# An expert stage of 72 tiles behind an attention stage: 24 of the tiles taken into the last attention steps

## The reference

```
h = [pos_table[pos], nest_table[nesting], seg_table[segments]] @ W        # embedding
h = h + attention(layernorm(h))       # chunks of 128 tokens, 8 heads of 64, feature map exp(q P - max)
h = h + moe(layernorm(h)):
    gates = softmax(x @ Wg + bg);  vals, idx = top_k(gates, 2);  vals /= sum(vals) + 0.01
    y_e = relu(x @ W1[e] + b1[e]) @ W2[e] + b2[e]                         # 8 experts, 128 -> 512 -> 128
    out = sum over the two chosen experts of vals * y_e
```

## Time and profile before

| | us |
|---|---|
| median of the three runs | 421.6 |
| profiled execution, span from first to last instruction | 438.2 |
| TensorE busy | 363.8 (83%) |
| VectorE busy | 313.1 (71%) |
| ScalarE busy | 253.5 (58%) |
| GpSimd busy | 244.2 (56%) |
| mean granted TensorE clock | 0.932 |

### The profile page before, as it was taken

How to read it: one execution, slowest core, us unless ns; L and a number is a source line. 1 busy time by engine, 2 the same in 40 slices (tenths; PEclk the granted TensorE clock), 3 DMA queues, 4 the chain that set the end, 5 groups by cost and what they waited for, 6 DMA issues and landing times.

```text
span 438.2 us, 12358 instructions
## 1 busy us (share of the span) xinstructions
PE 363.8 (83%) x3127; PEld 321.2 (73%) x3127; DVE 313.1 (71%) x1170; ACT 253.5 (58%) x705; POOL 244.2 (56%) x566
## 2 busy tenths in 40 slices
PE   1679999999999999999996435999999999999300
PEld 1457888787787877878885313999999999999300
DVE  7666878788777887777974561777777777678154
ACT  1246677776667676676754101777777777677200
POOL 6111117776667767677677660466666665766500
PEclk9989999999999999999999556999999999999855
DMA  5355500001000000000000031222222222221198
GB/s 136 92 158 159 155 1 21 21 15 31 27 27 13 13 27 27 27 20 13 20 28 28 28 101 48 61 74 73 77 71 76 70 75 70 70 76 58 54 308 243
DMA packets 39227, 29.54 MB, mean 67 GB/s; under 512 B 4679, under 2 KB 35778, under 8 KB 39202
## 3 DMA queue, kind: packets, MB, share of 16 engines
q1 hardware_dynamic: 27858, 16.30, 13.6%
q0 software_dynamic: 4352, 9.45, 6.0%
q10 hardware_dynamic: 6992, 3.50, 2.8%
HBM read 16.50 MB, written 12.73 MB: 67 GB/s over the span
## 4 chain that ended last, share of the span: by engine, by line
PE 63%; DVE 14%; DMA 8%; issue 6%; SPq 5%; DVEq 1%; POOL 1%; ACT 1%; another core or an unknown queue 0%; POOLq 0%; ACTq 0%
PE ps_out L1320 7%; PE ps_oy L1332 7%; PE ps_vc L1332 7%; PE ps_q L1320 6%; PE ps_k L1175 5%; PE ps_out L1213 4%; DMA row_of<-ids_dram 4%; PE ps_oy L1228 4%; PE ps_vc L1175 3%; SPq L480 3%; PE ps_oy L1221 3%; PE ps_q L1175 3%; PE ps_vc L1203 3%; PE ps_ln L1312 2%; PE ps_k L1320 2%
## 5 line engine op out<-in xcount | busy, mean ns | idle before, releaser
L607 POOL DMA_INDIRECT y_dram<-heads_out,place x72 | 73.8, 1025 | 29.9 <-issue 25.9
L578 POOL DMA_INDIRECT slots_dram<-rows,row_id x64 | 63.3, 988 | 19.5 <-issue 19.5
L734 ACT ACTIVATE k_prime<-ps_q,b_T 128x128 f32<-128x128 f32 x108 | 31.8, 365 | 19.8 <-PE ps_q L1320 19.8
L734 ACT ACTIVATE k_prime<-ps_out,b_T 128x128 f32<-128x128 f32 x108 | 31.8, 366 | 19.0 <-PE ps_out L1320 18.9
L544 POOL TENSOR_TENSOR rstd<-moments,ln_eps 128x2 f32<-128x2 f32 x32 | 6.2, 195 | 62.3 <-DVE moments L821 62.1
L1332 PE MATMUL ps_oy<-w_tile,k_prime 128*128 128x128 f32 x288 | 38.1, 275 | 0.4 <-issue 0.4
L1332 PE MATMUL ps_vc<-w_tile,k_prime 128*128 128x128 f32 x288 | 38.1, 275 | 0.1
L1320 PE MATMUL ps_out<-sT,w_tile 128*128 128x128 f32 x288 | 38.1, 275 | 0.0
L539 POOL TENSOR_TENSOR spare<-minus_half,ln_eps 128x2 f32<-128x2 f32 x89 | 18.1, 204 | 35.1 <-ACT heads_out L743 22.1
L1213 PE MATMUL ps_out<-context,qT 128*128 128x130 f32 x256 | 36.1, 283 | 1.5 <-issue 0.8
L1091 DVE COPY w_tile<-w_all 128x640 f32 x72 | 36.0, 499 | 1.5
(11 more groups left out here) (232 smaller groups left out, 1028.2 us busy)
## 6 DMA issues: line engine op xcount, KB each, us to landing
qkv_rows<-slots_dram SPq DMA_DIRECT2D x72, 72.0 KB
w_all<-in_L_ffn_W SPq DMA_DIRECT2D x1, 2048.0 KB, 13.5
w_all<-in_L_ffn_W SPq DMA_DIRECT2D x8, 256.0 KB, 4.6
y_first<-y_dram SPq DMA_DIRECT2D x8, 256.0 KB, 5.6
y_second<-y_dram SPq DMA_DIRECT2D x8, 256.0 KB, 6.0
out<-y_first ACTq DMA_DIRECT2D x8, 256.0 KB, 5.5
y_dram<-heads_out,place POOLq DMA_INDIRECT x72
slots_dram<-rows,row_id POOLq DMA_INDIRECT x64
```

Source lines behind the costliest of these rows:

```text
L578: nc.gpsimd.indirect_dma_start(slots_dram[:, :], bass.IndirectOffsetOnAxis(row_id[:, place_of(p, a), j, k:k + 1], 0), rows[:, place_of(p, ...
L607: nc.gpsimd.indirect_dma_start(y_dram[:, :], bass.IndirectOffsetOnAxis(place[:, a, :], 0), y[:, a, :], None).then_inc(s_placed[a], 16)
L734: last = nc.scalar.activation(hT[:, a % 2, c, :], ps_up[a % 2][0][:, c * P:c * P + P], ACT.Relu, bias=b1_T[:, bass.ds(experts[0] * FC + c, ...
```

## The change

The first 24 tiles of the expert stage (`EARLY = 4 * RING`) are placed from the counts after sequence 11 alone. Full tiles are a region's whole multiples of 128 rows; after 12 sequences there are 6144 choices, 48 tiles' worth, of which at least 41 tiles are full, whatever the routing. A first table (`early_counts`, `early_tiles`, `early_words`) is computed by DVE in steps 14 and 15; a second (`taken_tiles`, `later_counts`, `later_tiles`, `later_words`) places the other 48 tiles, from where the first left off in each region. `sequences` ends at `p = 15`. What steps 16 to 18 did is written out, on each engine, between the first steps of `slot_tile`, by `EarlyTiles`, which runs a given number of them at a time, unrolled. `pad` issues all eight padding DMAs on SP, between the load of tile 11 and that of tile 12; ACT issues none. SP waits for the scatters of sequences 12 to 15 and for the padding only ahead of tile 24. The transposed tile lands in `ps_qT` instead of `ps_ln`, the transposed b1 in `ps_q`. All warm-up matmuls of the expert stage are gone.

```diff
+    EARLY_SEQS = L1 - 2
+    EARLY = 4 * RING
+    LATER = FTILES - EARLY
...
-        for p in range(L1, SEQS + 3):
+        for p in range(L1, SEQS):
...
+    class EarlyTiles:
+        def __init__(self, eng, body, groups=None, known=None):
+            self.eng, self.body, self.groups, self.known = eng, body, groups, known
+            self.next, self.experts = -2, None
+        def run(self, count):
+            for n in range(self.next, self.next + count):
+                if n == EARLY - 2 and self.known is not None:
+                    self.eng.wait_ge(self.known, 2)
+                if n == -2 or n == EARLY - 2 or (n > 0 and n % RING == 0):
+                    self.experts = load_experts(self.eng, self.groups, max(n, 0) // RING)
+                self.body(n, n % RING, n // RING, self.experts(n - max(n, 0) // RING * RING))
+            self.next += count
+        def rest(self):
+            self.run(EARLY - self.next)
...
-        ps_slot, ps_y = ps_ln, (ps_oy, ps_vc)
+        ps_slot, ps_y = ps_qT, (ps_oy, ps_vc)
...
-            pad(sp, 0)
             sp.wait_ge(s_tiles, 1)
             firsts = [sp.value_load(tile_row[0:1, n:n + 1], min_val=0, max_val=SLOTS - P) for n in range(RING)]
-            sp.wait_ge(s_pad, 16 * E)
-            sp.wait_ge(s_empty, 16)
             for a in range(2):
-                sp.wait_ge(s_slots[a], 16 * 2 * TOP * SEQS // 2)
+                sp.wait_ge(s_slots[a], 16 * 2 * TOP * EARLY_SEQS // 2)
...
+            early = EarlyTiles(sp, load_ahead)
+            early.run(2 + RING)
+            pad(sp)
+            early.run(EARLY - 2 * RING)
+
+            sp.wait_ge(s_tiles, 2)
+            sp.wait_ge(s_pad, 16 * E)
+            sp.wait_ge(s_empty, 16)
+            for a in range(2):
+                sp.wait_ge(s_late[a], 16 * 2 * TOP * (SEQS - EARLY_SEQS) // 2)
+            early.rest()
             slot_tiles(sp, load_ahead)
...
+            early = EarlyTiles(pool, place_y)
+            q = SEQS - 3
+            weigh(q, q % 2)
+            pool.wait_ge(s_weighed, q + 1)
+            scatter(q, q % 2, last=1)
+            scale_and_shift(SEQS - 1, 1, moments2, rstd2, shift2, s_mom2, s_rstd2)
+            scatter(q, q % 2, first=1)
+            early.run(3)
+            pool.wait_ge(s_last_weighed, 1)
+            scatter(SEQS - 2, 0)
+            early.run(2)
+            pool.wait_ge(s_last_weighed, 2)
+            scatter(SEQS - 1, 1)
+            early.rest()
...
-            pad(act, 1)
...
+            act.wait_ge(s_groups, 1)
+            early = EarlyTiles(act, slot_tile, group_experts, s_groups)
+            early.run(2)
+            oT_copy(TILES - 1, 1)
+            act.wait_ge(s_late[0], 16 * 2 * TOP)
+            normalize_second(SEQS - 2, 0)
+            early.run(1)
+            x2T_copy(SEQS - 2, 0)
+            early.run(1)
+            normalize_second(SEQS - 1, 1)
+            early.run(1)
+            exps_of(SEQS - 2)
+            x2T_copy(SEQS - 1, 1)
+            early.run(2)
+            exps_of(SEQS - 1)
+            early.rest()
...
+            early = EarlyTiles(dve, slot_tile, group_experts, s_groups)
+            early.run(2)
+            ranks(SEQS - 3, 1)
+            early.run(1)
+            residual(TILES - 1)
+            dve.wait_ge(s_h2, TILES)
+            stats_of(SEQS - 1, stats2)
+            step.wait()
+            moments_of(1, stats2, moments2, s_mom2)
+            early.run(1)
+            gates(SEQS - 2)
+            early.run(1)
+            ranks(SEQS - 2, 0)
+            weigh_last(SEQS - 2, 0)
+            early.run(1)
+            gates(SEQS - 1)
+            early.run(1)
+            ranks(SEQS - 1, 1)
+            weigh_last(SEQS - 1, 1)
+            taken_tiles()
+            early.run(1)
+            later_counts()
+            early.run(1)
+            later_tiles()
+            early.run(1)
+            later_words()
+            early.rest()
...
-            warm_up(12, ps_qT[:, :])
-
...
-                if isinstance(n, int) and -1 <= n < 1:
-                    warm_up(2, ps_qT[:, :])
...
+            pe.wait_ge(s_b1_w, 16)
+            nc.tensor.transpose(ps_b1, b1_rows[:, :], ident[0:E * FC, 0:E * FC]).then_inc(s_b1, 1)
+            early = EarlyTiles(pe, slot_tile)
+            early.run(2)
+            pe.wait_ge(s_b1r, 1)
+            rank_product(SEQS - 3)
+            o_transpose(TILES - 1, 1)
+            early.run(1)
+            y_product(TILES - 1, 1)
+            x2_transpose(SEQS - 2, 0)
+            pe.wait_ge(s_h2, TILES)
+            early.run(1)
+            gate_product(SEQS - 2, 0)
+            early.run(1)
+            rank_product(SEQS - 2)
+            x2_transpose(SEQS - 1, 1)
+            early.run(1)
+            gate_product(SEQS - 1, 1)
+            early.run(1)
+            rank_product(SEQS - 1)
+            early.rest()
             slot_tiles(pe, slot_tile)
```

More of the change, by code:

```diff
@@ L106, in sequences, with load_experts, taken_out, experts @@
             step.base, step.count = start + per * ((L1 - L0) // 2), 0
-        for p in range(L1, SEQS + 3):
+        for p in range(L1, SEQS):
             body(p, p % 2, p // 2)
+    def load_experts(eng, groups, group):
+        if groups is None:
+            return lambda at: None
+        word = eng.value_load(groups[0:1, span(group, 1)], min_val=0, max_val=E ** DIGITS - 1)
+        taken = {}
+        def taken_out(at):
+            if at not in taken:
+                taken[at] = eng.snap((word >> (E_BITS * at)) & (E - 1))
+            return taken[at]
+        def experts(at):
+            return [taken_out(k) if 0 <= k < DIGITS else None for k in range(at, at + 3)]
+        return experts
@@ L130, in load @@
[L130 to L134, removed]
+            return load_experts(eng, groups, group)
         start = step.base + step.count if step else 0
-        with eng.Fori(1, FTILES // RING - 1) as i:
+        with eng.Fori(EARLY // RING, FTILES // RING - 1) as i:
             experts = load(i)
             if step:
-                step.base, step.count = start + (i - 1) * per, 0
+                step.base, step.count = start + (i - EARLY // RING) * per, 0
@@ L144, in slot_tiles @@
         if step:
[L145 removed]
+            step.base, step.count = start + per * (FTILES // RING - 1 - EARLY // RING), 0
         first = FTILES - RING
@@ L374, in lm_tower_kernel @@
         s_slots = [sem(f"rows_in_slots{a}") for a in range(2)]
+        s_late = [sem(f"late_rows_in_slots{a}") for a in range(2)]
+        s_b1_w = sem("b1_rows_in")
         s_w1, s_w2 = sem("w1_of_tile_ready"), sem("w2_of_tile_ready")
@@ L1021, in weigh_last, with ranks, gates @@
                                         ALU.add).then_inc(s_last_weighed, 1)
+            def ranks(p, a):
+                read_ranks(p)
+                step.wait()
+                move_next_row()
+                rows_of_choices()
+                step.wait()
+                give_rows(p, a)
+            def gates(p):
+                read_logits(p)
+                dve.wait_ge(s_lgr, p + 1)
+                find_top()
+                step.wait()
+                find_top_ids()
+                below_top()
+                step.wait()
+                choose(p)
@@ new lines, in later_tiles, with later_words @@
+            def later_tiles():
+                experts_of(tiles_to, LATER)
+                nc.vector.tensor_tensor(tile_row[:, EARLY:FTILES], first_f[:, 0:LATER], later_row[:, :], ALU.add)\
+                    .then_inc(s_tiles, 1)
+            def later_words():
+                step.done(nc.vector.tensor_scalar(tile_expert[:, EARLY:FTILES], expert_f[:, 0:LATER], float(E - 1), None,
+                                                  ALU.min))
+                dve.wait_ge(s_groups, 1)
+                words_of(EARLY // RING - 1, FTILES // RING)
@@ L1026, in sequence @@
                 even(p, a)
+                if isinstance(p, int) and p == L1:
+                    early_counts()
+                if isinstance(p, int) and p == L1 + 1:
+                    early_words()
                 odd(p, a)
-                if isinstance(p, int) and p - 2 in LAST:
-                    weigh_last(p - 2, a)
+                if isinstance(p, int) and p == L1:
+                    early_tiles()
             dve.wait_ge(s_row_head, 16 * PARTS)
```

166 lines of the change are left out of this document (93 added, 73 removed).

## The result

The changed kernel takes 409.1 us (median of 4 runs, 408.5 to 409.8) beside 421.3 us (420.7 to 424.4) for the kernel before on the same chip: a ratio of 0.967, 95% interval 0.963 to 0.971. The forecast was 410.0 us. The span of its profiled execution is 407.4 us, and each timed run is 1.7 to 1.8 us longer than its span.

A forecast was written before the change was run, and what follows sets the result against it. DVE was taken to bind the mixed stretch: 240.3 + 32.4 + 2.4 + 2.0 puts tile step n = 10 at 277.1, gaining 13.0 us. 421.6 − 13.0 + 1.4 gives 410.0 us, range 401 to 418.

The forecast's parts named there:

- What bounds, and the ceiling: TensorE bounds the expert stage, nothing is full around the seam; removing the seam's 34 us could gain 29 us at most.
- The start, 2.0 us late: Early table parts in steps 14 and 15: 4.3 us added to DVE, 2.3 covered, so step 15 ends 2 us later.
- DVE's sum, 32.4 us: DVE's queue from step 15's end: 15.7 us of pieces, nine tiles at 13.5, weight copies and register reads; DVE binds.
- Idle from the relay, 2.4 us: Mixed stretch: waits in the relay that don't line up leave DVE idle 2.4 us, bounds 0 and 8.
- The clock, 2.0 us: TensorE's clock falls again near the seam; half speed costs little while DVE binds: 2.0 us added, bounds 0 and 5.
- Padding on SP, 8.9 us, no cost: SP alone issues eight padding DMAs in 8.9 us; tile 12's load lands at 276.1, needed at 279.0: no cost.
- GpSimd, no cost: Eight late scatters between result placings of tiles 0, 2 and 3; GpSimd catches up by tile 8: no cost.
- From the profile to the metric, 1.4 us off: Profiled span is 16.6 us over the median; part may lie in the seam, so 1.4 us is taken off the gain.
- TensorE at half clock: Rival: TensorE stays at half clock through the mixed stretch and bounds it; gain 8, about 414 us; chance 0.10.
- Fuller overlap: Rival: no idle, late start or clock loss in the mixed stretch; gain 19.4, time 402 to 404 us; chance 0.10.
- The chain: Rival: the hand-written order makes relay and tiles wait for each other, stretch over 49.8 us; 426 or more; chance 0.06.
- an effect of the profiler: Rival: no measurable change, as the seam was mostly made by the profiler, all 16.6 us; 418 to 424; chance 0.06.

The follow-up runs named there:

- the second trace of the kernel before: The kernel before, no edit, profiled a second time: 424.8 us, ratio 1.003, span 422.0 us where its first trace had 438.2.
- the two-queue run: The changed kernel with the eight padding DMAs split, four issued by ACT behind its sixth tile and four by SP: 411.9 us, ratio 0.974.
- the first four experiments: Kernel before again, 424.8 us; changed kernel with relay ahead of the tiles, 414.2, padding on two queues, 411.9, or padding twice, 420.2.

## Why the prediction was right

Forecast 410.0, measured 409.1. The mechanism held: relay and tiles overlap and DVE sets the pace. That the number is so near is luck, as two errors all but cancel. Worked with the recipe of the prediction on the second trace of the kernel before, n = 10 would have come at 227.7 + 2.0 + 36.8 = 266.5, which answers to tile 1's up product at 249.4, and that was at 257.6: a gain of 8.2. The traces give 422.0 − 407.4 = 14.6. The difference, 6.4, is made of the terms below: 1.4 at the start and 5.0 in the stretch.

- **What bounds, and the ceiling**: held. The seam was the place, the gain lies in it; tiles run at 1.9 us behind it and 28.6 us follow TensorE's end (378.8 to 407.4), in both traces before.
- **The start, 2.0 us late**: 0.6. The mask is at 228.12 against 227.52. Counted from the mask one sequence earlier it is 0.9 (228.12 − 216.96 = 11.16 us against 227.52 − 217.28 = 10.24). The early parts took DVE some 3.8 us, so they found about 3 us of cover, where I had counted 2.3.
- **DVE's sum, 32.4 us**: 30.8. From the mask's end at 228.29 to n = 10's up product at 260.09 it is 31.8, 1.0 of it idle (0.65, 0.18, 0.20). To the end of `later_words` (258.53) it is 30.2, under the 33 to 37 that I had named as the sign; these group words stand ahead of step n = 8, not of n = 9 as I wrote. That DVE is the bound is shown by the table run twice: 2.2 us added, 2.2 us of wait. The two register reads, priced at 1.2 and 0.7, show as 1.05 and 1.16.
- **Idle from the relay, 2.4 us**: 1.0. TensorE's waits of 8.3 us are the other side of DVE's full queue.
- **The clock, 2.0 us**: nothing; the granted clock is 1.00 in all rows. That wasn't sure to be so: with later padding it fell to half at 252.17, with the padding one at a time behind 252.50, though TensorE's and DVE's programs up to there are the changed kernel's. From the mask to n = 10 it was 31.9 and 32.1 us there against 32.0 here, so my reason, that half speed costs little while DVE binds, held where a fall came. The Trainium skill, "TensorE: Matmul & The Clock Gate", Part 1, lets idling lower the clock; here seven waits up to 2.03 us didn't, a wait of 1.88 us did in another run, and so did a relay with nothing between (0.63).
- **Padding on SP, 8.9 us, no cost**: 8.04, no cost, but for a wrong reason. I took it that two queues share a limit; the two-queue run shows none. The 7.91 us of the earlier trace rows belonged to an unusual execution (3.75 in the second trace). And the slack was 1.0 us, not 2.9, as the doubled padding shows: from `pad_at` (249.35) to the transpose of tile 12 (261.88) it is 12.5 us, where I had 14.5. The Trainium skill, "DMA: Bandwidth & Descriptors", Issuing engines are not separate DMA queues, which says that several issuers save only issue time, describes what the two-queue run shows: 3.6 us twice, side by side.
- **GpSimd, no cost**: held in the changed kernel. Missed was that its late scatters and their landing, not table and padding, end the seam in the second trace before; in the first, SP's padding was a link, as I had read it. The gain has a part that the prediction doesn't price: the first loads no longer wait for them.
- **From the profile to the metric, 1.4 us off**: the premise was false. Of the 16.2 us that the first trace was longer, 10.6 lay ahead of the mask, 8.9 of them in the attention loop, which is full of TensorE's work and which I had taken as one that can't be shorter, 4.8 in the seam and 0.8 behind. The gain to expect of the seam was smaller by 4.8, not 1.4. This and the overestimated stretch all but cancelled: 13.0 − 4.8 + 6.4 = 14.6.

**The rivals.** Padding at 2.0 us each and TensorE at half clock didn't occur. Fuller overlap nearly did in its conditions (idle 1.0, start 0.6, no loss by the clock), on a seam that was 4.8 us shorter than it assumed; so its 402 to 404 didn't come. The chain needed a stretch over 49.8 us; it took 31.8. Of "an effect of the profiler", 4.8 us of the first trace's seam are missing in the second; that the profiler made them is not shown. The timed gains were 12.2 us on the first chip and 14.4 on another; why the kernel before took 2 us more there and the changed one didn't is open. Its 18 runs beside the first four experiments lie between 419.6 and 425.6, so a median of four can be off by as much.

## What to carry to other kernels

When a serial relay stands between two dense stages, move work that needs none of its results into it, then sum the queue of the engine that both share: the pace is that engine's, and here a piece added to it cost its full length. Lay its pieces over as many tiles as there are, so that the spare time of the tiles between them (about 0.4 us each here, 1.9 less DVE's 1.5) makes up for each, and put no block longer than the ring's lead in any queue that feeds the ring. If a profiled execution is several per cent longer than the median, take another one before pricing anything by it.

## What the runs showed of the hardware

- A padding DMA whose address is read into a register took 0.9 to 1.0 us to issue on SP and on ACT, each at its own pace; first loads, with registers read beforehand, 0.5 us (six in 3.01).
- Behind TensorE waits of 4.01, 5.76 and 8.17 us the clock was at half, and within 1 us behind one of 4.31. Behind waits of 1.83 and 1.88 us it fell too, behind others of 1.78, 1.88 and 2.03 it didn't: where TensorE's program up to there was the same, it fell in two executions and stayed in four. What tells them apart is open.
- One execution of the kernel before ran its attention loop with 847 matmuls in 100 us, another with 917, both at the full clock. The cause wasn't found.
